# Latent attention on one core: the rotary query's high and low parts in an earlier unit of each slot of the second chunk

## The reference

```python
q_pe = apply_rope(q[..., NOPE:], cos, sin)
q_lat = jnp.einsum('bshd,hdc->bshc', q_nope, wkv_b_h[:, :NOPE])
kv_cache = rmsnorm(kv_lat, kv_norm_w)
scores = (jnp.einsum('bshc,btc->bsht', q_lat, kv_cache)
          + jnp.einsum('bshr,btr->bsht', q_pe, k_pe)) * SCALE
scores = jnp.where(causal[None, :, None, :], scores, NEG_INF)
attn = jax.nn.softmax(scores, axis=-1)
out_lat = jnp.einsum('bsht,btc->bshc', attn, kv_cache)
out = jnp.einsum('bshc,hdc->bshd', out_lat, wkv_b_h[:, NOPE:])
return out.reshape(B, S, N_HEADS * VDIM) @ wo.T
```

## Time and profile before

| | us |
|---|---|
| median of 3 timed runs | 1771.49 |
| lowest and highest of them | 1764.94, 1775.77 |
| profiled execution | 1764.38 |
| its span | 1762.6 |
| PE busy (share of the span) | 1662.0 (94%) |
| DVE busy | 1180.8 (67%) |
| POOL busy | 963.4 (55%) |
| ACT busy | 820.1 (47%) |

### The profile page before, as it was taken

How to read it: one execution, slowest core, us unless ns; L and a number is a source line. 1 busy time by engine, 2 the same in 40 slices (tenths; PEclk the granted TensorE clock), 3 DMA queues, 4 the chain that set the end, 5 groups by cost and what they waited for, 6 DMA issues and landing times. The chain is left out here.

```text
span 1762.6 us, 27068 instructions
## 1 busy us (share of the span) xinstructions
PE 1662.0 (94%) x9030; PEld 1396.0 (79%) x9030; DVE 1180.8 (67%) x2755; ACT 820.1 (47%) x1295; POOL 963.4 (55%) x595
## 2 busy tenths in 40 slices
PE   6778999899999999999999999999999999999996
PEld 5567777677777777788888888888888888888885
DVE  6546777666776766677677777677766677676763
ACT  4334444434444453444445444455454444545452
POOL 4554444435555554555556565565656465656554
PEclk9899999999999999999999999999999999999998
DMA  7666887747666666475555555657656556555553
GB/s 275 253 221 205 273 272 231 246 125 198 177 165 167 168 179 193 129 208 153 158 138 154 164 151 162 195 153 188 158 141 165 129 152 160 145 149 135 147 130 103
DMA packets 117375, 309.08 MB, mean 175 GB/s; under 512 B 28786, under 2 KB 29299, under 8 KB 115956
## 3 DMA queue, kind: packets, MB, share of 16 engines
q1 hardware_dynamic: 89008, 227.04, 44.8%
q10 hardware_dynamic: 28228, 80.31, 16.4%
HBM read 113.25 MB, written 34.60 MB: 84 GB/s over the span
## 5 line engine op out<-in xcount | busy, mean ns | idle before, releaser
L1394 POOL TENSOR_TENSOR pT<-pT,pT_h 128x1024 fp32r<-128x1024 f32 x320 | 689.2, 2182 | 423.5 <-ACT pT_h L1283 421.6
L1141 DVE TENSOR_SCALAR_CACHE_REDUCE probs<-p_score 128x512 f32<-128x512 f32 (+3 forms) x640 | 380.9, 601 | 337.7 <-PE p_score L1065 217.3
L1262 ACT ACTIVATE probs<-probs,neg_max 128x128 f32<-128x128 f32 (+15 forms) x256 | 307.5, 1201 | 409.2 <-DVE neg_max L1147 334.8
L1283 ACT ACTIVATE pT_h<-pT 128x1024 fp32r<-128x1024 f32 x320 | 291.3, 964 | 232.7 <-PE p_out L1085 177.3
L1163 DVE STREAM_TRANSPOSE turned<-probs 128x1024 f32<-128x1024 f32 (+7 forms) x384 | 341.6, 915 | 40.7 <-ACT probs L1262 36.1
L1085 PE MATMUL p_out<-pT_h,V_h 128*128 128x256 f32 (+3 forms) x1024 | 299.7, 293 | 12.9 <-POOL pT L1394 12.9
L1085 PE MATMUL p_out<-pT,V_h 128*128 128x256 f32 (+3 forms) x1024 | 302.6, 295 | 0.0
L1085 PE MATMUL p_out<-pT_h,V_l 128*128 128x256 f32 (+3 forms) x1024 | 302.1, 295 | 0.0
L1065 PE MATMUL p_score<-Kp,qp_h 128*128 128x512 f32 (+3 forms) x640 | 236.4, 369 | 14.2 <-POOL qp_l L1386 14.0
L1065 PE MATMUL p_score<-Kn_h,q_h 128*128 128x512 f32 (+3 forms) x640 | 242.7, 379 | 2.0 <-DVE q_l L1186 1.7
L1065 PE MATMUL p_score<-Kn_l,q_h 128*128 128x512 f32 (+3 forms) x640 | 234.0, 366 | 0.0
(11 more groups left out here) (123 smaller groups left out, 2095.5 us busy)
## 6 DMA issues: line engine op xcount, KB each, us to landing
pT<-turned SPq DMA_DIRECT2D x384, 128.0 KB, 3.4
Wq<-wq_scr ACTq DMA_DIRECT2D x63, 512.0 KB, 4.3
Wv<-wv_scr SPq DMA_DIRECT2D x63, 512.0 KB, 4.2
pT<-turned SPq DMA_DIRECT2D x192, 112.0 KB, 3.9
pT<-turned SPq DMA_DIRECT2D x192, 96.0 KB, 2.5
pT<-turned ACTq DMA_DIRECT2D x128, 128.0 KB, 3.9
Wp<-wp_scr SPq DMA_DIRECT2D x31, 512.0 KB, 4.9
pT<-turned SPq DMA_DIRECT2D x192, 80.0 KB, 2.8
```

The lines of the kernel that those rows point to most:

```text
L1141: dve.tensor_scalar(probs[row % ROW_RING][:, b * CW:b * CW + width], p_score[n % SCORE_RING][:, 0:width], SCALE, LOWEST, ALU.mult, ALU.max ...
L1262: act.activation(probs[row % ROW_RING][:, 0:width], probs[row % ROW_RING][:, 0:width], ACT.Exp, bias=neg_max[p][:, i:i + 1], scale=1.0, ac ...
L1283: act.activation(high.rearrange("p r t i q -> p r t (i q)"), low.bitcast(F32).rearrange("p r t i q -> p r t (i q)"), ACT.Copy).then_inc(p_ ...
L1394: pool.tensor_tensor(low.rearrange("p r t i q -> p r t (i q)"), low.bitcast(F32).rearrange("p r t i q -> p r t (i q)"), high.bitcast(F32). ...
```

## The change

The unit of the two steps high_rotary (ACT) and low_rotary (POOL) changes in the second chunk (phase 1). In slots of even heads, where the head to come is odd, it is u = 2 (third unit) instead of 5 (sixth). In slots of odd heads, where the head to come is even, it is u = 4 (fifth unit), in slot 31 u = 5 (sixth) instead of 6. Nothing else is different; within the unit the steps keep their place in each engine's order.

```diff
 def rotary_high_unit(s):
     if phase(s) == 2:
         return 1 if not opens_head(s) else None
-    return rotary_unit(s) + (2, 5, None, 5)[phase(s)] if opens_head(s) else None
+    if phase(s) == 1 and head_of(s) % 2 == 0:
+        return 2
+    return rotary_unit(s) + (2, 4, None, 5)[phase(s)] if opens_head(s) else None
```

## The result

The changed kernel takes 1758.94 us in the median of 6 runs (1751.37 to 1760.94), against 1770.05 us (1764.94 to 1775.77, 6 runs) before: a ratio of 0.9938 with a 95% interval of 0.9913 to 0.9962. Two later comparisons on other chips gave 0.9957 (0.9936 to 0.9978) and 0.9966 (0.9952 to 0.9980). Pooled, the means are 1766.5 us before (the 75 runs of the later comparisons; 1766.8 with the six of the first) and 1759.0 us changed (all 30 runs): the change brings 7.5 us, 0.4%.

What follows compares the result with a forecast made beforehand. TensorE (PE) was taken to set the pace. Border stalls of 11.2 us, less 1.15 swallowed, plus 0.4, gave 10.4 us off the 1771.49 median: 1761.1 us, range 1753 to 1768; a gain of 8.5 to 12.6 had chance 0.70.

Steps and rivals of the forecast that it cites:

- What stops PE at the borders: Between heads, PE waits 14.8 us for `qp_l` and `q_l`, late behind `high_rotary`; removing these waits gives 11.2 us.
- the border behind slot 31: Border after the chunk's last slot, 1.6 us idle: a gain of 0.4 us, bounds 0.6 gained or 0.4 lost.
- the five steps: Last projection product to the first score tile's last product: 2.12 us (odd) and 1.70 (even), 1.14 without a stop.
- The covers: Moved copies cost 0: ACT's 3.07 us idle hides them in even slots, 0.8 us on DVE in odd slots.
- The wait for `Wv` keeps its size: DVE's chain moves 0.92 us where PE moves 0.98, so the load of `Wv` comes only 0.06 later relative to PE.
- rival A: The load of `Wv` takes the even slots' gain, leaving 6.2 us: 1758.2 profiled, 1765.3 against the median; chance 0.12.
- The first value group is a fixed arrival: Chunk start: two borders' gain, 1.2 us idle, is swallowed by the 1.8 us stop for the first value group.
- The last border is swallowed, 0.4 us: Chunk end: the last border's gain, 0.4 us idle, is swallowed by the 3.2 us stop for the next chunk's `xT`.
- What would show it: In the chunk, `qp_l` and `q_l` waits nearly go and two slots take about 40.2 us; wrong if near 41.7.

Runs made afterwards that it cites:

- e6: Kernel before, with the query's rotary parts behind high_query, in the seventh unit of every second-chunk slot: 1767.79 us, ratio 1.0018.
- e10: Changed kernel, with the query's rotary parts in the fifth unit in even slots too, instead of the third: 1759.54 us, ratio 0.9957.
- e5: Kernel before, with the load of Wv issued ahead of the exchange from the second chunk's fourth slot on: 1764.83 us, ratio 0.9989.
- e4: Changed kernel, with the load of Wv issued ahead of the last row's exchange from the second chunk's fourth slot on: 1751.56 us, ratio 0.9906.
- e7: Changed kernel, with the load of Wv cut to 64 KB instead of 512 from the second chunk's fourth head on: 1749.68 us, ratio 0.9908.
- e3: Kernel before, with only the change's half for odd slots (fifth unit, slot 31 sixth): 1765.79 us, ratio 0.9991.
- e9: Changed kernel measured a third time, no edit, 12 runs: 1758.92 us, ratio 0.9966.
- e2: Kernel before, with only the change's half for even slots (third unit): 1762.16 us, ratio 0.9971.
- e8: e4, with the load of xT issued ahead of the next Wq at each change of chunk: 1745.51 us, ratio 0.9886.

## Why the prediction was right, and where its sum was not

The time lies where it was forecast (1758.94 against 1761.1). That it lies so near is in part luck: the median of three runs that the forecast started from, 1771.49, is 5.0 us above the mean of the 75 later ones, and the gain was forecast 2.9 us too large. The pooled gain of 7.5 us is below the 10.4 forecast, and below the lower bound of 8.5 that had the chance of 0.70. The mechanism at the borders was right; the other stops and the clock were not.

*What stops PE at the borders.* Right. The waits of PE for both operands went from 14.8 us to 0.4, 0.7 and 0.6 in the three profiles (372 to 704 us; 0.4 of each is at the border behind slot 31), the five steps to 1.14 us, DVE's idle before `q_l` from 15.6 us in 15 waits to 1.5 in two. The covers held: the even slot's copies end before the exponential, and `high_output` in the odd slot is not felt. e6 and e10 confirm which chain it was: the place ahead of `high_query`. The border behind slot 31 lost 0.97 us instead of 1.44, a gain of 0.47 where 0.4 was forecast.

*The wait for `Wv` keeps its size.* Wrong; this is rival A in part. I had read that DVE's chain moves 0.92 us where PE moves 0.98, and that `Wv` falls behind by 0.06. In most even slots PE wanted `Wv` 11.9 us after the end of DVE's last transpose of the head before. Changed, it is 11.7 in some, and 11.0 to 11.4 in four or five of the seven even slots from 18 to 30 (before in one or two). The second kind comes from a link that my steps had left out. ACT and DVE in the changed kernel, at the change to slot 24:

```profile
534.12 2.96 ACT L1285 ACTIVATE pT_h<-pT 128x1024 fp32r<-128x1024 f32 x3 [1.42 <-DMA pT<-turned]
```

```profile
538.24 1.25 DVE L1165 STREAM_TRANSPOSE turned<-probs 128x1024 f32<-128x1024 f32 x1 [0.80 <-ACT probs L1264]
```

ACT now reaches the value groups before the exchange has landed and waits in its queue. The last row's exponential stands behind them, the transpose waits for it, and with the transpose the next exchange and the load of `Wv` start late. Relative to PE they lose another 0.7 us there. The stops for `Wv` from slot 18 on went from 3.9 and 4.0 us to 7.4, 6.7 and 4.1, 2.1 us more on the mean (in slot 17 they are 0.5 us less).

This link is not the whole of it. The largest piece, 1.8 of the 2.1 us, is slot 28, where PE did not stand before and stands 1.5 to 2.1 us in all three profiles. There the margin is 11.7 us, so the link is absent, but the load took longer: 6.9, 7.6 and 7.5 us to land, against 5.1 and 4.8 before. The stop, and the landing, in the changed kernel's first profile:

```profile
631.97 0.70 PE L1099 MATMUL p_result<-Wv,o_h 128*128 128x512 f32 x2 [1.38 <-issue]
...
DMA to landing us min/median/max: 6.9/6.9/6.9
```

Over the even slots from 18 to 28 the landings are 5.8 us on the mean before and 6.0 changed, so this is one slot and not a general slowing. Why it is this slot stays open, and no run takes the link on ACT away by itself. And the stop in an even slot's middle no longer shortens the one at its end (e5), so all of it counts.

I gave rival A 6.2 us as the gain that is left. The pooled gain of 7.5 lies between that and the forecast. That the load of `Wv` limits the changed kernel's slots is shown by e4 and e7; e4 shows what it holds back: 8 us, clock included. The Trainium skill, "DMA: Bandwidth & Descriptors", section "Issuing engines are not separate DMA queues", has it that transfers of all queues interleave. Here the same load landed in 4.3 to 8.5 us behind the exchange and in 3.3 to 5.0 us ahead of it (e4), which agrees: all transfers together moved some 1.2 MB during the short landings behind the exchange (4.8 us in slot 26) and 1.8 MB during the long ones (7.5 us in slot 28).

*The first value group is a fixed arrival.* Not borne out. Counted from the start of the chunk, PE's product for it came at 62.3 and 63.4 us before and at 59.7, 59.5 and 58.7 changed, and the stop ahead of it kept its size (1.8 and 3.4 us, then 2.9, 2.7 and 2.1). What the prediction took off for these two borders, 0.9 us, was not swallowed there.

*The last border is swallowed, 0.4 us.* Mis-sized. The `xT` stop was 3.2 and 1.6 us before, and 4.2, 5.9 and 5.4 changed: 2.8 us more on the mean, 0.4 forecast. PE comes to it about 1 us sooner after the load's issue (the border and the stop for `Wv` that lie between are shorter), and the load itself took 9.9, 11.4 and 10.9 us, before 9.8 and 8.2.

*The clock.* Left out altogether. I had taken a us of stop for a us of time. One stretch of the changed kernel, PE and then the granted clock (0.5 would be 1.2 GHz throughout):

```profile
468.26 0.70 PE L1099 MATMUL p_result<-Wv,o_h 128*128 128x512 f32 x2 [2.09 <-issue]
```

```profile
460.00:468.00 8.00, 6.17 (x33) 4.93 (x31) 4.33 (x11) 3.25 (x6) 2.58 (x2) 1.00 1.02 248
468.00:472.00 4.00, 3.74 (x11) 2.70 (x12) 1.45 (x3) 1.96 (x3) 0.83 (x1) 0.66 0.17 57
472.00:476.00 4.00, 4.00 (x17) 3.29 (x16) 3.48 (x6) 2.12 (x4) 4.00 (x3) 0.91 0.00 0
```

The clock is at 2.4 GHz through the stop, then below it in both stretches that follow: 0.66 of 4 us and 0.91 of 4 us are 2.7 and 0.7 us at 1.2 GHz, 3.4 in all. PE does half of its work in that time, so the stop of 2.1 us costs another 1.7. Within the chunk 6.8 and 3.4 us stood at 1.2 GHz before, and 13.7, 17.1 and 10.2 changed. Of the 8.5 us more on the mean, 6.3 stand at the stop for `xT` and 2.3 at stops for `Wv`. Some of it costs nothing, since PE stands still in it anyway: 0 and 0.2 us before, 1.1, 4.2 and 2.3 changed. So PE worked 6.2 us longer at 1.2 GHz, and half of that, 3.1 us, is what the clock cost in the chunk.

The timed executions bear it out, in which the mean granted clock is known: 59.3 us at 1.2 GHz on the mean before (75 runs), 65.4 changed (30 runs). If PE was at work all that time, their times at full clock would be 1736.9 and 1726.3 us. That would be 10.6 us gained, of which 3 are paid back by the clock. As PE stood still in 2.4 us more of it in the profiled chunks, an estimate from these numbers is rather 9.3 gained and 1.8 paid back. That this comes near the forecast's 10.4 is in part luck: the sum below shows it as a larger gain at the borders less stops that grew. e3's timed runs show the same pattern: 3.7 us gained at full clock, and 67.1 us at 1.2 GHz against 61.1 in the kernel before beside it. In its profile only 3.4 us of the chunk are at 1.2 GHz, so where the rest stands is not shown.

What turns one stop into such a stretch and spares another was not settled: in e3's profile stops of 2.2 and 2.5 us passed without one, in e9's one of 1.7, while in e2's a stop of 2.6 was followed by one. The Trainium skill, "TensorE: Matmul & The Clock Gate", section "What's actually happening", names the same two levels and has the clock set by how busy PE has been recently; the order of events here agrees (the stop ends at 468.3, the clock falls at 469.3), but the stops without such a stretch are not explained by it.

*The balance of the chunk.* Borders -11.2; `Wv` +1.6 (2.1 less the 0.5 of slot 17), `xT` +2.8, value groups +0.1 (3.2 to 3.3 on the means), clock +3.1: -3.6. The profiles show -4.9. Two slots without any other stop lost 2.31 us (41.74 to 39.43), while their borders account for 2.09; that is 1.7 us over the chunk, which I have traced to no row. With it the sum is -5.3, and the 0.4 that is left is within the scatter of the changed kernel's chunk.

*What would show it.* Two slots: 40.2 us forecast, 41.2, 41.2 and 40.0 measured on the mean, 39.43 undisturbed. The prediction called itself wrong if two slots stay near 41.7 us; in two of the three profiles they lie nearer to that than to 40.2. The forecast had the right direction for each sign but was too sure that the other stops keep their size.

## What to carry to other kernels

Before a stop on the bounding engine is counted as a gain, look for the other stops in the same slot: where two waits are released by different things, the slot loses the longer one, and removing one brings only the difference (e5: 1 to 2 us for an edit that brings 8 once the other stop is gone). Ask of every load whose place in a queue was chosen behind other transfers whether its own release came earlier. And where an engine's clock can fall behind a stop, as here in some cases, the stop costs more than its own length; what that adds is to be read from rows at the lower clock in which the engine works.

## What the runs showed of the hardware

A stop of TensorE of 1.9 to 2.1 us in an otherwise busy stretch was followed by 3.4 us at 1.2 GHz in two of three profiles of the changed kernel, while stops of 2.2 and 2.5 us in e3 were not; I had not reckoned with the clock at all. After a stop PE's first product was followed by the next in 0.31 to 0.34 us instead of 0.23. The same 512 KB load took 4.3 to 8.5 us from issue to landing behind eight 128 KB transfers in the changed kernel, and 3.3 to 5.0 us ahead of them in e4 (3.3 to 5.1 in e8, and 3.4 to 4.4 in e5 but for one of 6.2). The time ahead of the second chunk scattered by 5.6 us (371.5 to 377.0) among 13 profiles of kernels that don't differ there.
